# A stationary operand read straight from blocks of 32 features, instead of from a plain copy of them

## The reference, cut to what matters

```python
for _ in range(T):                                   # T = 3
    a_in = einsum('nm,bmd->bnd', in_mat, h)          # in_mat = out_mat = adj
    a_out = einsum('nm,bmd->bnd', out_mat, h)
    av = concatenate([a_in, a_out])
    z = sigmoid(lin(av, w3) + lin(h, u3))
    r = sigmoid(lin(av, w4) + lin(h, u3))
    hv = tanh(lin(av, w5) + lin(r * h, u5))
    h = (1 - z) * h + z * hv
```

## Time and profile before

| | before |
|---|---|
| median of three runs | 882.19 us |
| the profiled execution's own time | 881.74 us |
| its span in the profile | 880.0 us |
| TensorE (PE) busy | 863.4 us, 98% |
| VectorE (DVE) busy | 743.9 us, 85% |
| ScalarE (ACT) busy | 492.5 us, 56% |
| GpSimd (POOL) busy | 124.4 us, 14% |

### The profile page before, as it was taken

The page is one execution under the profiler, slowest core; times in us unless marked ns, Lnnn a source line. Parts: engine busy times, 40 slices in busy tenths (PEclk is TensorE's granted clock), DMA queues, the critical chain, the costliest instruction groups (busy, mean ns, idle before and its releaser), DMA issues.

```text
span 880.0 us, 19328 instructions
## 1 busy us (share of the span) xinstructions
PE 863.4 (98%) x7356; PEld 706.8 (80%) x7356; DVE 743.9 (85%) x1518; ACT 492.5 (56%) x881; POOL 124.4 (14%) x161
## 2 busy tenths in 40 slices
PE   8999999999999999999999999999999999999997
PEld 7868888787888878878788788888888788788885
DVE  5988889888898888888988788888889888898666
ACT  5565655656456564665645646456554556555553
POOL 1110112101131020310112101120111301121000
PEclk9999999999999999999999999999999999999999
DMA  6013323623344243451424614155232543234222
GB/s 187 24 50 121 97 96 114 189 83 105 110 141 156 66 137 104 145 168 49 144 72 145 190 51 143 49 168 168 83 110 75 176 134 97 97 114 127 73 72 96
DMA packets 88451, 99.53 MB, mean 113 GB/s; under 512 B 8640, under 2 KB 80576, under 8 KB 88384
## 3 DMA queue, kind: packets, MB, share of 16 engines
q1 hardware_dynamic: 88384, 98.50, 35.3%
HBM read 50.76 MB, written 47.71 MB: 112 GB/s over the span
## 4 chain that ended last, share of the span: by engine, by line
PE 49%; DVE 18%; issue 12%; DMA 11%; ACT 5%; SPq 3%; POOL 2%; DVEq 0%; ACTq 0%; POOLq 0%
PE cand L438 8%; PE gate L438 7%; PE gate L433 5%; PE gate L434 5%; PE gate L435 5%; PE fea L590 3%; DMA h_back<-h_trip 3%; DVE c_s L1184 3%; PE cand L433 3%; PE cand L434 3%; PE cand L435 3%; DMA hx_trip<-hx 2%; DVE a_lo L990 2%; SPq L252 2%; DMA h_trip<-h_turned 2%
## 5 line engine op out<-in xcount | busy, mean ns | idle before, releaser
L864 ACT ACTIVATE r_s<-gate,b_r 128x512 f32<-128x512 f32 x96 | 60.7, 684 | 89.2 <-PE gate L438 89.1
L770 ACT ACTIVATE h_hi<-h 128x512 fp32r<-128x512 f32 x92 | 57.0, 630 | 67.9 <-DVE h L990 46.1
L770 ACT ACTIVATE rh_hi<-rh 128x512 fp32r<-128x512 f32 x96 | 58.9, 632 | 47.4 <-DVE rh L1216 47.4
L378 POOL TENSOR_TENSOR rstd<-vare,minus_half 128x4 f32<-128x4 f32 x32 | 41.6, 1301 | 292.6 <-DVE vare L1024 292.6
L433 PE MATMUL gate<-h_hi,W_hi_u 128*128 128x512 f32 x192 | 80.1, 417 | 0.2 <-DVE h_lo L990 0.2
L877 ACT ACTIVATE z_s<-gate,b_z 128x512 f32<-128x512 f32 x96 | 62.9, 681 | 28.2 <-PE gate L435 28.2
L1216 DVE TENSOR_TENSOR rh<-r_s,h 128x512 f32<-128x512 f32 x96 | 67.4, 743 | 10.4 <-ACT r_s L864 9.9
L433 PE MATMUL gate<-a_hi,W_hi_wz 128*128 128x512 f32 x192 | 74.8, 390 | 0.6 <-DVE W_lo_wz L990 0.6
L434 PE MATMUL gate<-h_lo,W_hi_u 128*128 128x512 f32 x192 | 75.2, 392 | 0.0
L435 PE MATMUL gate<-h_hi,W_lo_u 128*128 128x512 f32 x192 | 75.1, 391 | 0.0
L438 PE MATMUL cand<-rh_hi,W_hi_u 128*128 128x512 f32 x188 | 74.9, 398 | 0.0
(11 more groups left out here) (160 smaller groups left out, 2034.2 us busy)
## 6 DMA issues: line engine op xcount, KB each, us to landing
h_back<-h_trip SPq DMA_DIRECT2D x216, 128.0 KB, 2.8
h_trip<-h_turned SPq DMA_DIRECT2D x40, 512.0 KB, 2.6
x_s<-x SPq DMA_DIRECT2D x15, 512.0 KB, 5.1
out<-o_s SPq DMA_DIRECT2D x15, 512.0 KB, 3.9
hx_back<-hx_trip SPq DMA_DIRECT2D x56, 128.0 KB, 2.8
h_trip<-h_blk SPq DMA_DIRECT2D x14, 512.0 KB, 3.2
hx_trip<-hx SPq DMA_DIRECT2D x14, 256.0 KB, 3.3
hx_trip<-hx SPq DMA_DIRECT2D x28, 128.0 KB, 3.2
```

The lines of the kernel that those rows point to most:

```text
L378: nc.gpsimd.tensor_tensor(rstd[n][:], vare[n][:], minus_half[:], ALU.pow).then_inc(rstd_ready[n], 1)
L770: return nc.scalar.activation(dst, src, ACT.Copy)
L864: nc.scalar.activation(r_s[:, c, :], gate[:, c, :], ACT.Sigmoid, bias=b_r[:, c:c + 1]).then_inc(r_ready, 1)
```

## The change

`t_s`, its semaphore `t_ready` and ScalarE's `take_back` go. A second form of the product, `adjacency_of_blocks`, is used in windows 1 to 4: it waits for the loads of `h_back` itself and takes one block of 32 features at a time as the stationary operand, 64 nodes x 32 features, with the same 64x64 moving operand. The output of a matmul is 32 partitions of a bank. There are 2 x 4 x 4 x 2 = 64 matmuls in place of 32. The order is half c, quarter q, block b, graph e.

```diff
-            def adjacency(src, n, t_full=None):
+            def adjacency_of_blocks(n, w):
                 fea_wait(n, 1)
-                for c in range(C):
-                    if t_full is not None:
-                        pe.wait_ge(t_ready, t_full + c)
+                pe.wait_ge(h_in, 16 * BL * w)
+                for c in range(C):
+                    for q in range(Q):
+                        for b in range(BL):
+                            for e in range(2):
+                                last = nc.tensor.matmul(set_bank(e)[b * K:(b + 1) * K, c, q, :], h_back[half(e), b, q, c, :],
+                                                        adjT[half(e), half(e)], start=True, stop=True)
+                last.then_inc(fea_full, 2)
...
-                    adjacency(t_s, use("adj %d" % k), 8 * i + 2 * k - 1)
+                    adjacency_of_blocks(use("adj %d" % k), w)
...
-            def take_back(w):
-                act.wait_ge(h_in, 16 * BL * w)
-                for c in range(C):
-                    copy(t_s[:, :, c * P:(c + 1) * P].rearrange("p q (b f) -> p q b f", b=BL),
-                         h_back[:, :, :, c, :].rearrange("p b q f -> p q b f")).then_inc(t_ready, 1)
...
-                if k == 3:
-                    take_back(w)
-                    update_sigmoid(w)
-                else:
-                    update_sigmoid(w)
-                    if k in (1, 2, 4):
-                        take_back(w)
+                update_sigmoid(w)
```

More of the change, by code:

```diff
@@ L113, in gated_graph_kernel @@
         h_back = sb("h_back", [P, BL, Q, C, K])
-        t_s = sb("t_s", [P, Q, D])
         r_s = sb("r_s", [P, C, T])
@@ L187, in gated_graph_kernel @@
         tok_taken = sem("tok_taken")
-        h_is_turned, h_out, h_in, t_ready = sem("h_is_turned"), sem("h_out"), sem("h_in"), sem("t_ready")
+        h_is_turned, h_out, h_in = sem("h_is_turned"), sem("h_out"), sem("h_in")
         final_ready = sem("final_ready")
@@ L579, in transpose_last, with adjacency @@
                     last.then_inc(tok_full, 1)
-            def adjacency(src, n, t_full=None):
+            def adjacency_of_blocks(n, w):
+                fea_wait(n, 1)
+                pe.wait_ge(h_in, 16 * BL * w)
[6 more added lines that the diff above has]
+                last.then_inc(fea_full, 2)
+            def adjacency(src, n):
                 fea_wait(n, 1)
                 for c in range(C):
-                    if t_full is not None:
-                        pe.wait_ge(t_ready, t_full + c)
                     for q in range(Q):
```

## The result

The changed kernel takes 889.58 us, the median of five runs (887.73 to 891.28); the kernel before takes 882.19 (879.82 to 883.83 in five runs beside it). The ratio is 1.0084, with a 95% interval of 1.0064 to 1.0103. That is 7.4 us slower, outside what I called the likeliest (878.5 to 883, no change), inside the whole range, and within 0.5 us of the rival called the middle price (890), to which I gave one chance in ten.

What follows compares the result with a forecast made beforehand. It took TensorE, busy 98% of the span, to bound the kernel. Product +0.9, waits for `t_s` -1.15 and window 3 -0.83 sum to -1.1 us, giving 880.8 us; likeliest 878.5 to 883, whole range 878 to 911.

Steps and rivals of the forecast that it cites:

- the likeliest: The forecast's own case for the whole kernel: 880.8 us, within 878.5 to 883, chance 0.50.
- the whole range: The widest span given for the kernel's time, reaching to the slow rival: 878 to 911 us.
- the middle price: Rival, product in windows 1 to 4: bursts 10 ns apart or instruction fetching, +10 us, 890 us; chance 0.10.
- TensorE bounds the kernel, ScalarE has room: Whole kernel: TensorE busy 98% of the span, ScalarE 56%; in late windows TensorE's own stream is the time.
- The product, "+0.9 us": Product in windows 1 to 4: eight places start eight pairs per unchanged 0.06 us period; 32 x 0.028 = +0.9 us.
- TensorE's waits for `t_s`, "-1.15 us": Product in windows 1: five late starts behind ScalarE's copy all go, 5 x 0.23 = -1.15 us.
- Window 3, "-0.83 us": One window 3: without the copy ahead of the sigmoid, the late `a_lo` matmul at 430.71 comes on time, -0.83 us.
- Waits that a longer product swallows: Late `a_lo`: a longer product gives them more room, some 2.9 us remaining; lowers the slow rival's 910.4 to 907.5.
- The slow rival: Product in windows 1 to 4: eight places sustain only a pair per 15 ns, +30.7 us, 909 us; chance 0.28.

Runs made afterwards that it cites:

- e4: Kernel before, with every 64x64 matmul of the product in windows 1 to 4 made twice (128 records on four places): 904.81 us, ratio 1.0248.
- e5: Changed kernel with the product cut in four parts of 32 pairs, two 512-column matmuls between them: 912.2 us, ratio 1.0338 to the kernel before.
- e7: e6 with ScalarE's copy put back in its old place, into a tile that is not read: 881.77 us, ratio 0.9998 to the kernel before.
- e6: Kernel before without the copy: 32 matmuls, 64 stationary columns from two adjacent runs in `h_back`, weights reordered in DRAM; 879.6 us, ratio 0.9967.
- e1: Kernel before, ScalarE's copy kept, with only the product in windows 1 to 4 cut into 64 matmuls of 64x32: 889.69 us, ratio 1.0081.
- e3: Changed kernel with a moving operand of 32 columns in place of 64 in windows 1 to 4: 884.86 us, ratio 1.0025 to the kernel before.
- e8: Changed kernel with only two of the four quarters multiplied in windows 1 to 4 (64 records): 878.99 us, ratio 0.9969 to the kernel before.
- e9: Changed kernel with block b outside quarter q, eight records in a row on the same two places: 919.19 us, ratio 1.0414 to the kernel before.

## Why the prediction was wrong, step by step

- **TensorE bounds the kernel, ScalarE has room.** Right, and the sharper for it: the late windows grew by just the 0.32 us of the product.
- **The product, "+0.9 us": the step that failed.** I wrote that the array waits for the place, not for instructions, and that eight start per period. That held for 32 pairs. Of the 128, the last 95 come behind a pause of 0.085 us at 10 ns a pair, and a product takes 1.27 us between its first and last start in place of 0.94: 32 x 0.32 = +10.3 us where I had +0.9. The counts of the earlier trace rows could not show it: at 15 ns a pair four places never ask for more than the supply gives, and e4 shows them at it without a break. I had read a burst of four as a sustained rate.
- **The middle price** had the right size, 0.32 us a product, from another cause: a spacing of 10 ns within a burst. It is 7 ns, so that its 890 came so near to 889.58 is in good part luck. It also named the fetching of instructions. 74 packets were brought in place of 58, but they are not what is slow: in 23 of the 32 products of the changed kernel no packet of instructions was on its way, and the break is at the same pair in all. The product at 817.71 is one of them (the last two columns of its counts, the share and the rate of DMA, are 0.00 and 0). So if it is the supply, its slow part lies behind the packets.
- **A cost I left out.** Behind the product the weighted sum starts 0.14 us after the start of the last record in place of 0.04, in 14 windows: +1.5 us, the change of tile form (e5).
- **TensorE's waits for `t_s`, "-1.15 us".** They went: the product starts 817.71 - 817.16 = 0.55 us behind the last pair, as undisturbed, in every window. But e7, which has only this of the relief, has no gain that can be measured, and its loop is only 0.4 us shorter. Part of it went into the waits for `a_lo`: inside the loop they sum to 2.9 us in e7 and to 2.45 before.
- **Window 3, "-0.83 us".** The wait at 430.71 went in e6, but the sum of the waits for `a_lo` stayed 2.8 us, and the loops of e6 and e7 are equally long. So what ScalarE's time is worth (2.2 us by the medians) did not come by this way. In the changed kernel it is worth nothing (e1), because its longer products let `a_lo` come in time anyway: one late `a_lo` of 0.68 us is left in the loop, where five were before.
- **Waits that a longer product swallows.** I used them for the slow and the middle rival and not for the sum. The added work is 10.3 + 1.5 = 11.8 us, the kernel is 7.4 slower: 4.4 us were swallowed, relief and slack together. e1 has the slack without the relief and the same time, so the slack is enough.
- **The slow rival** (30 us) was wrong in its bound: 128 pairs do not keep the old rate of 15 ns, they reach 10. Of the two mechanisms that it named, a limit in the stream of instructions is the one that fits the runs.

## What to carry to other kernels

When a change doubles the number of small matmuls, ask two rates of the trace: how long one place of the array is held, and how fast instructions come when more than 64 of them are wanted in a row; a burst seen between pauses says nothing on the second. A product that stays on fewer, wider operands is worth a reordering of the features in the weights: the same relief of ScalarE without more matmuls in the loop gave 0.9967 (0.9955 to 0.9979) in place of 1.0084. And where TensorE is 98% busy, its remaining waits are still slack for what you add, and come back for what you take away.

## What the runs showed of the hardware

- Pairs of load and matmul on free places start 7 ns apart; 32 of them, eight places in turn, start in 0.24 us. Behind them came a pause of 0.085 us (0.11 in e3), then 9 to 10 ns a pair, in the changed kernel, e1, e3 and e8. Two large matmuls between parts are enough to start anew (e5).
- Going into and out of tiled matmuls costs 0.36 us beside the matmuls themselves, and changing from 64x32 to 64x64 0.11 us (e5).
- The order in which matmuls visit the places matters as much: the same 128 records start over 1.27 us with eight places in turn and over 2.24 us with two repeated (e9). Two starts came in 0.035 us there on the mean, which is not explained.
